# A transformer layer on eight cores: four weight loads at the heads of stages waited for in parts, one part moved to another queue

## The reference

```python
q = x @ Wq;  k = x @ Wk;  v = x @ Wv                      # 2048 x 2048 each
scores = (q.T @ k) / 8                                     # over features: 2048 x 2048
attn = (softmax(scores, -1) @ v.T).T @ Wo
x = layernorm(x + attn)
w1_q = sign(w1) * (abs(w1) >= 0.7 * mean(abs(w1)))         # 8192 x 2048, values -1, 0, 1
w2_q = sign(w2) * (abs(w2) >= 0.7 * mean(abs(w2)))         # 2048 x 8192
h = gelu(x @ w1_q.T + b1)                                  # 2048 x 8192
x = layernorm(x + h @ w2_q.T + b2)
```

## Time and profile before

| | us |
|---|---|
| median of 3 timed runs | 3876.92 |
| lowest and highest of them | 3569.8, 4032.92 |
| the profiled execution | 3568.61 |
| its span, slowest core (core 5) | 3567.1 |
| spans of the eight cores | 3530.3 to 3567.1 |
| TensorE busy | 3181.1 |
| VectorE, ScalarE, POOL busy | 1240.8, 730.8, 94.4 |

### The profile page before, as it was taken

One profiled execution on the slowest core, in us unless ns is written; L12 is line 12 of the kernel. 1 busy time (PEld: TensorE's weight loads), 2 busy tenths in 40 slices (PEclk: granted clock), 3 DMA queues, 4 the chain that ended last, 5 costly groups with the idle time before them and its releaser, 6 DMA issues.

```text
span 3567.1 us, 37244 instructions; the slowest of 8 cores (3530.3 to 3567.1 us)
## 1 busy us (share of the span) xinstructions
PE 3181.1 (89%) x14917; PEld 1443.1 (40%) x14917; DVE 1240.8 (35%) x1362; ACT 730.8 (20%) x1065; POOL 94.4 (3%) x166
## 2 busy tenths in 40 slices
PE   0897898995995996997999999999969999899997
PEld 0343343442442442443444444444424444344443
DVE  0111221112555960555343433434313333333333
ACT  1345455230111221455111111111100000200003
POOL 0000000000000000000000000000000000000000
PEclk9999999997997998998999999999989999899998
DMA  9899998575457753665656655555563233723322
GB/s 197 216 272 287 256 276 275 156 220 116 142 155 234 267 187 83 218 234 176 186 184 203 180 192 191 188 193 187 175 241 142 82 131 138 244 90 142 122 91 95
DMA packets 357613, 656.83 MB, mean 184 GB/s; under 512 B 177152, under 2 KB 234560, under 8 KB 332864
## 3 DMA queue, kind: packets, MB, share of 16 engines
q1 hardware_dynamic: 239392, 302.05, 26.3%
q0 software_dynamic: 41648, 184.60, 18.8%
q10 hardware_dynamic: 76400, 167.79, 14.3%
HBM read 536.98 MB, written 150.99 MB: 193 GB/s over the span
## 4 chain that ended last, share of the span: by engine, by line
PE 49%; DMA 2%; ACT 1%; issue 0%; DVE 0%; ACTq 0%; DVEq 0%; SPq 0%
PE psH L974 25%; PE psF L1074 23%; DMA y<-outt 1%; DMA w2g<-w2q_h 1%; PE psF L1068 0%; ACT lnsink L1154 0%; DVE outt L1099 0%; DMA w1sl<-w1q_h 0%; DMA h_h<-hstg 0%; ACT mr_t L1176 0%; ACT st L1163 0%; DVE oacc L1124 0%; ACT hstg L991 0%; ACT ve_t L1166 0%; ACT rstd_t L1174 0%
## 5 line engine op out<-in xcount | busy, mean ns | idle before, releaser
L974 PE MATMUL psH<-big,w1sl 128*128 128x512 bf16 x4096 | 887.0, 380 | 11.7 <-DMA w1sl<-w1q_h 11.7
L1074 PE MATMUL psF<-w2g,hg 128*128 128x512 bf16 x4096 | 891.5, 380 | 0.0
L974 PEld LDWEIGHTS psH<-big,w1sl 128*128 128x128 bf16 x4096 | 401.4, 98 | 497.0 <-issue 15.5
L1074 PEld LDWEIGHTS psF<-w2g,hg 128*128 128x128 bf16 x4096 | 400.6, 98 | 490.6 <-issue 13.9
L1124 DVE TENSOR_TENSOR oacc<-psF,oacc 128x2048 f32<-128x2048 f32 x112 | 256.5, 2291 | 573.9 <-PE psF L1074 573.9
L450 ACT ACTIVATE sbin<-sbin 128x1024 f32<-128x1024 f32 x256 | 268.9, 1051 | 418.8 <-DMA sbin<-w1t 192.7
L319 PE MATMUL psA<-wbuf,big 128*128 128x512 bf16 x1024 | 227.6, 384 | 111.5 <-DMA wbuf<-wq 100.3
L229 DVE TENSOR_TENSOR qout<-qmask,qout 128x1024 bf16<-128x1024 f32 x256 | 311.5, 1218 | 0.0
L991 ACT ACTIVATE hstg<-psH,b1sb 128x2048 bf16<-128x2048 f32 x64 | 125.9, 1967 | 745.1 <-PE psH L974 745.1
L696 PE MATMUL psO<-big,atsl 128*128 128x512 bf16 x1024 | 226.8, 383 | 45.9 <-DMA big<-v_h 25.2
L319 PE MATMUL psB<-wbuf,big 128*128 128x512 bf16 x1024 | 227.7, 384 | 21.7 <-DVE spillb L365 21.7
(11 more groups left out here) (115 smaller groups left out, 1333.3 us busy)
## 6 DMA issues: line engine op xcount, KB each, us to landing
w2g<-w2q_h SPq DMA_DIRECT2D x16, 4096.0 KB, 13.4
sbin<-w2t SPq DMA_DIRECT2D x76, 512.0 KB, 6.5
sbin<-w1t SPq DMA_DIRECT2D x64, 512.0 KB, 8.4
sbin<-w1t ACTq DMA_DIRECT2D x64, 512.0 KB, 9.4
qin<-w1t POOLq DMA_DIRECT2D x32, 1024.0 KB, 7.4
w1q_h<-qout SPq DMA_DIRECT2D x64, 512.0 KB, 3.4
w1sl<-w1q_h SPq DMA_DIRECT2D x64, 512.0 KB, 7.2
qin<-w2t POOLq DMA_DIRECT2D x32, 1024.0 KB, 8.7
```

Source lines behind the costliest of these rows:

```text
L974: mm = t.matmul(ps[:, nb * 512:nb * 512 + 512], w1sl[:, (f_m % 2) * 2048 + d_k * P: (f_m % 2) * 2048 + d_k * P + P], big0[:, d_k * S + nb ...
L1074: mm = t.matmul(ps[:, nb * 512:nb * 512 + 512], hg[:, slot * 8192 + f_k * 1024 + j * P: slot * 8192 + f_k * 1024 + j * P + P], w2g[:, slot ...
```

## The change

Four edits of one kind, and a moved load:

1. p1: each of the eight Wq and Wk blocks comes as two DMAs of eight e_k each, into the same places. The streams g_wq and g_wk get four semaphores each. TensorE waits for the first DMA ahead of a block and for the second ahead of e_k 8 of its first tile.
2. p4: the wait for both Wo loads ahead of e_k 8 becomes a wait for the first there and one for the second ahead of e_k 12. The loads stay as they are.
3. f2: SP's load of W2 group 0 covers f_k 0 to 3 only (2 MB).
4. f2: the other half (f_k 4 to 7, into columns 8192 to 16383 of w2g) is issued by ScalarE's queue behind the hg load of group 0, on stream s_misc as item 1; ScalarE waits for all quantised spills (c_wq) first.
5. f2: TensorE waits for s_misc item 1 ahead of f_k 4 of its first tile.

```diff
--- before.py
+++ after.py
@@ -118,7 +118,7 @@
         strm = lambda name, k=2: DStream(stx, nc, name, k)
 
         g_xfm = strm("g_xfm"); g_id = strm("g_id", 1)
-        g_wq = strm("g_wq"); g_wk = strm("g_wk")
+        g_wq = strm("g_wq", 4); g_wk = strm("g_wk", 4)
         g_wo = strm("g_wo"); g_wo2 = strm("g_wo2")
         s_stats = strm("s_st", 5); s_qsl = strm("s_qsl"); s_vre = strm("s_vre", 4)
         s_osl = strm("s_osl"); s_x = strm("s_x"); s_x2i = strm("s_x2i", 8)
@@ -283,9 +283,13 @@
                             nb = i % 4
                             if i >= 2:
                                 g.wait_ge(t_q.h, 16 * (i - 1))
-                            st_w.issue(
-                                g, wbuf[:, (i % 2) * 8192:(i % 2) * 8192 + 8192],
-                                hap(w, nb * 512, [[E, P], [P * E, nE], [1, 512]]))
+                            for h in range(2):
+                                st_w.issue_idx(
+                                    g, wbuf[:, (i % 2) * 8192 + h * 4096:
+                                            (i % 2) * 8192 + h * 4096 + 4096],
+                                    hap(w, nb * 512 + h * 8 * P * E,
+                                        [[E, P], [P * E, 8], [1, 512]]),
+                                    2 * (i % 4) + h)
                         g.wait_ge(t_q.h, 144)
                         for j in range(2):
                             g_wo.issue(
@@ -308,7 +312,7 @@
                         g_xfm.wait_all(t)
                         for i in range(8):
                             st_w = g_wq if i < 4 else g_wk
-                            st_w.wait_item(t, i % 4)
+                            st_w.wait_item(t, 2 * (i % 4))
                             half = wbuf[:, (i % 2) * 8192:(i % 2) * 8192 + 8192]
                             for s_m in range(nS):
                                 ti = i * nS + s_m
@@ -316,6 +320,8 @@
                                     t.wait_ge(v_ev.h, ti - 7)
                                 pv = qk_view(ti % 8)
                                 for e_k in range(nE):
+                                    if s_m == 0 and e_k == 8:
+                                        st_w.wait_item(t, 2 * (i % 4) + 1)
                                     mm = t.matmul(
                                         pv,
                                         big0[:, e_k * S + s_m * P:e_k * S + s_m * P + P],
@@ -803,7 +809,9 @@
                                     t.wait_ge(v_z.h, max(0, 4 * s_m - 2))
                                 for e_k in range(nE):
                                     if s_m == 0 and e_k == 8:
-                                        g_wo2.wait_all(t)
+                                        g_wo2.wait_first_n(t, 1)
+                                    if s_m == 0 and e_k == 12:
+                                        g_wo2.wait_first_n(t, 2)
                                     wsrc = wbuf if e_k < 8 else wobuf2
                                     wof = (e_k % 8) * E
                                     for nb in range(4):
@@ -1025,9 +1033,15 @@
                             sy.wait_ge(t_f.h, (gi - 1) * nhalf)
                         c_h.wait_first_n(sy, 8 * (g + 1))
                         slot = gi % 2
-                        s_w2g.issue(
-                            sy, w2g[:, slot * 16384:slot * 16384 + 16384],
-                            hap(w2q_h, (g * 8) * P * E, [[E, P], [P * E, 8], [1, E]]))
+                        if gi == 0:
+                            s_w2g.issue_idx(
+                                sy, w2g[:, 0:8192],
+                                hap(w2q_h, 0, [[E, P], [P * E, 4], [1, E]]), 0)
+                        else:
+                            s_w2g.issue_idx(
+                                sy, w2g[:, slot * 16384:slot * 16384 + 16384],
+                                hap(w2q_h, (g * 8) * P * E,
+                                    [[E, P], [P * E, 8], [1, E]]), gi)
                         if gi > 0:
                             s_hg.issue_idx(
                                 sy, hg[:, slot * 8192:slot * 8192 + 8192],
@@ -1070,6 +1084,8 @@
                                                  b2bf[:, nb * 512:nb * 512 + 512],
                                                  start=True, stop=False)
                                 for f_k in range(8):
+                                    if gi == 0 and j == 0 and f_k == 4:
+                                        s_misc.wait_item(t, 1)
                                     for nb in range(4):
                                         mm = t.matmul(
                                             ps[:, nb * 512:nb * 512 + 512],
@@ -1139,9 +1155,13 @@
                 @blk.scalar
                 def _(s):
                     c_h.wait_all(s)
+                    c_wq.wait_all(s)
                     s_hg.issue_idx(
                         s, hg[:, 0:8192],
                         hap(h_h, 0, [[S, P], [P * S, 8], [1, 1024]]), 0)
+                    s_misc.issue_idx(
+                        s, w2g[:, 8192:16384],
+                        hap(w2q_h, 4 * P * E, [[E, P], [P * E, 4], [1, E]]), 1)
                     nm_col = [st6[:, 4 + 2 * (k % 2):5 + 2 * (k % 2)] for k in range(2)]
 
                     def ln2_stats(hj):
```

## The result

| | before | changed |
|---|---|---|
| median of 29 timed runs each | 3574.86 | 3584.66 |
| lowest | 3564.04 | 3572.05 |
| the profiled execution | 3568.61 | 3576.0 |
| its span, slowest core | 3567.1 (core 5) | 3574.5 (core 3) |
| ratio | | 1.0037, 95% interval 1.0025 to 1.0050 |

The kernel became slower by 0.37%, 13 us of 3570, and that is clear of the scatter: the interval does not reach 1. It is within 2%, and 3584.66 lies inside the range from 3558 to 3590, but the forecast rise was 6.9 us and the measured one is about twice that. (Some executions, two of the three behind the 3876.92 shown ahead of the prediction among them, are disturbed: the cores of one die, or of both, get a lower clock; the ratio goes by the others, whose medians are 3567.24 and 3580.20.)

The account below looks back on a forecast made before the run. TensorE, 89% busy and with its matmuls on the chain, was taken to bound the kernel. The terms -2.0 (p1), -3.6 (p4) and +12.5 (f2) sum to +6.9 on 3568.6, giving 3575 us, range 3558 to 3590.

Parts of the forecast that it names:

- What bounds the kernel, and what can be won: TensorE's matmuls bound the kernel; p1, p4 and f2 can each win at most about the time of a few matmuls.
- Part 1: p1: TensorE starts on half the first Wq block, runs 8 matmuls, waits 3.1 us; -2.0 us (0 to -3.4).
- the two cases of the restart: p1 after the wait: TensorE returns at the lower clock level, winning 1.7 us, or does not, winning 3.4.
- Part 2: p4: 16 matmuls start on Wo's first load, then a 6.6 us wait and a second restart; -3.6 us.
- Part 3: f2: start no earlier, then a 10.4 us wait for W2's second part; +12.5 us (+9 to +16), all carried through.
- start of 220 packets against 30: f2 before the change: ScalarE's queue was 220 packets ahead against SP's 30 before the two took turns packet by packet.
- B: Rival, f2: queues share by bytes once 8 KB rows meet 2 KB rows; f2 -0.5, sum -6.1, 3562.5 us; chance 0.12.
- C: Rival: all three edits pay, the second queue adding flow; f2 -7.5, sum -13.1, 3555.5 us; chance 0.06.
- D: Rival, f2: SP's full queue crowds out ScalarE's second load; f2 +35.9, sum +30.3, 3599 us; chance 0.07.
- E: Rival: later waits swallow the gains of p1 and p4, f2's loss stands; +12.5, 3581 us; chance 0.07.
- The sign: Whole kernel: slower, by 6.9 us; chance 0.97 of staying within 2%.
- A: The forecast itself: f2's wait costs more than p1 and p4 give; 3568 to 3582 us; chance 0.68.

Follow-up runs that it names:

- halves: Changed kernel with W2's second part in SP's queue ahead of oacc, h in two loads, no c_wq wait on ScalarE; ratio 0.995 against the kernel before.
- cwq_late: Changed kernel with ScalarE's wait for c_wq put between its h load and its second W2 load; ratio 1.0017 against the kernel before.
- oacc_2k: Changed kernel with each of the eight oacc loads cut into four of 512 columns (2 KB rows); f1's end to f2's second tile 38.7 us, no ratio.
- oacc_held: Changed kernel with SP's oacc loads issued only when W2's second part has landed; ratio 0.9956 against the kernel before.
- w2_all_sp: Changed kernel with W2's second part in SP's queue ahead of oacc and no c_wq wait on ScalarE; ratio 0.9984 against the kernel before.
- before_cwq: Kernel before with ScalarE's wait for c_wq added ahead of its h load; f1's end to f2's second tile 39.6 us against 36.8, no ratio.

## Why the prediction was right or wrong

**What bounds the kernel, and what can be won: right.** The heads of p1 and p4 gave about the time of their few matmuls and no more, and f2's gives 6.8 us in halves, where its first 20 matmuls take 7.7 (core 3, 1.86 + 5.87). The extra wait came inside L1074 (now L1090) for w2g, as forecast.

**Part 1, right as far as it can be seen.** Start on core 5 at 94.46 (forecast 93.7), then 8 matmuls, a wait of 2.45 us (3.1), and a set of 56 matmuls in 13.66 us, between the two cases of the restart (12.2 would be the full pace of the earlier trace rows):

```profile
94.46 3.57 PE L325 MATMUL psA<-wbuf,big 128*128 128x512 bf16 x8 [94.46 <-DMA wbuf<-wq]
100.48 13.66 PE L325 MATMUL psA<-wbuf,big 128*128 128x512 bf16 x56 [2.45 <-DMA wbuf<-wq]
```

The gain at the second set is 1.9 us, or 2.4 over all kernels (forecast 2.0). Its way to the end is open, as said.

**Part 2, right.** Waits 10.0 and 6.5 (8.5 and 6.6), both restarts paid (6.47 and 5.14 us for 16 matmuls, forecast 5.6 each), -3.1 us against -3.6.

**Part 3, the step that failed: "The added wait for the quantised spills (c_wq) on ScalarE costs nothing."** I argued that SP has the same wait and issues only 0.1 us later, and did not see that this 0.1 us, by which ScalarE was ahead, was the "start of 220 packets against 30" that I used two paragraphs above. The added wait puts ScalarE level with SP or behind it, and the start falls to SP: 57 packets of h against 130 of W2 by 2585. The rest of the working holds. Put these counts into it: W2's first part has 512 - 130 = 382 rows left, 382 x 0.294/16 = 7.0 us, to 2592.0 (its landing came 2.3 us later, at 2580.9 + 13.4 = 2594.3). h has 1024 - 57 - 382 = 585 left, now beside 8 KB rows, 585 x 0.485/16 = 17.7 us, to 2609.7; it landed at 2580.9 + 28.9 = 2609.8. W2's second part, 512 x 0.575/16 = 18.4 us, to 2628.1; it landed at 2581.4 + 46.1 = 2627.5. For the two landings that TensorE waits for, the count of rows that go in turn is thus good to 1 us. With the start that it had before, h would have landed after 22.5 us by my sum; cwq_late, with the start given back, has 24.2. The f2 term was mis-sized by 6.3 us: 18.8 for 12.5. Of these, 5.8 are the later first matmul, and 0.5 two sets that ran a little longer (on core 5, bias and first half 7.3 us for 7.1, second half 6.0 for 5.6). cwq_late takes back 4.9 of the 5.8. The other 0.9 stay with the start given back: the sum was short for h by 1.7 us there, and why is open.

The wait inside the tile was forecast as 10.4 us and is 10.3 on core 5. That is no luck of cancelling: h and the second W2 part stand in one queue, so when h is late, both are.

**The rivals.** B fell by the landings (W2's first part at 13.4 us and h at 28.9, not together) and by oacc_2k. C fell too: both queues together moved 324 GB/s from 2594 to 2610, no more than SP's alone (342 in the earlier trace rows). D, that ScalarE's second load is held, did not happen: its issue took 0.62 us, and its rows followed h's at once. E is half open, as p1 is.

**The sign** was right, and the forecast of no change by 2% too; the range for A alone, 3568 to 3582, holds the 3580.20 of the undisturbed executions near its upper end. That is luck. f2's term of 18.8 lies outside the +9 to +16 from which that range was built; what made up for it are the gains of p1 and p4 (5.0 by the trace, where its upper end has 3.1) and a median before that lies 1.4 us below the profiled 3568.6.

## What to carry to other kernels

Before moving a load to another queue, list what will stand *beside* it, row by row: two busy queues take turns by rows, so a queue of 2 KB rows next to one of 8 KB rows got 23% of the bytes here, and one of 4 KB rows 36%. Keep the rows that the first tile doesn't need behind all that it does need, in *both* queues. Then a wait in two parts pays, whether both operands are cut at the same place (halves) or the residual loads are held back (oacc_held). And a wait that is already met is not free when two queues start together: ask who issued first before, and who does after.

## What the runs showed of the hardware

Two queues on the same 16 DMA engines moved rows one for one over whole stretches, with rows of 2, 4 and 8 KB. On core 5 of the changed kernel, 2594 to 2610 us, with 2 KB rows in q10 and 8 KB rows in q1 (packets, MB, share):

```profile
q1 hardware_dynamic: 553, 4.01, 75.7%
q10 hardware_dynamic: 555, 1.18, 23.9%
```

h got 1.18 of 5.19 MB, 23%. From 2612 to 2624 us, with 4 KB rows in q10, it was 1.53 of 4.20 MB, 36%:

```profile
q1 hardware_dynamic: 373, 2.67, 62.9%
q10 hardware_dynamic: 373, 1.53, 37.9%
```

With 2 KB rows in q1 (oacc_2k, core 5, 2598 to 2615.5 us, where W2's 4 KB rows come first in q1 and then in q10):

```profile
q1 hardware_dynamic: 1163, 3.04, 53.0%
q10 hardware_dynamic: 1168, 2.67, 47.4%
```

I had not expected how much an issue a tenth of a microsecond earlier brings. In the first 4 us the earlier queue moved 227 rows against 23 (cwq_late, 0.10 us ahead), and with 0.01 us the other way 57 against 130. This start is kept for the whole of the load: between the two kernels 277 rows change sides, (227 - 23) + (130 - 57). By the forecast's 0.383 us for an 8 KB row that would be 6.6 us of h's landing; 4.7 were measured.

The moment of the issue is not the whole of it; the size of the load that goes first counts too. With ScalarE 0.10 us ahead, its lead 4 us after the issue was 175 to 217 packets over the eight cores where h's load has 1024 rows (w2_all_sp), and 105 to 119 where its first load has 512 (halves), with W2 in loads of 512 rows in both. With SP 0.01 us or less ahead it was 104 to 125 for a W2 load of 1024 rows (before_cwq) and 71 to 77 for one of 512 (changed). Why that is so, no run here shows.

Nor do the eight cores load alike. In each of the 13 traces and in each pair of cores (0 and 1, 2 and 3, 4 and 5, 6 and 7), the core that ended f1 later had the longer first wait in f2: 27.9 against 24.2 us in the kernel before, 34.2 against 29.6 in the changed one (means of four cores each). What the two cores of a pair share, no run here separates.
